# Sorting the edges of a four-layer graph network: message weights from bf16 parts, one group later, on one core

## The chip, the cores and the metric

The kernel runs on 1 core of one Trainium2 chip. The metric is the device time of one execution in microseconds (us), lower is better. The engines are TensorE (PE in the profile, its weight loads PEld), VectorE (DVE), ScalarE (ACT), GpSimd (POOL) and SyncE (SP), and DMA queues are fed from SP, ACT and POOL.

## The reference, cut to what matters

The graph has 6250 nodes of 64 features and 200000 edges. Four layers follow one another, each added to its input and normalised.

```python
# layer 0: per edge a weight of 64 numbers from a two-layer MLP on 8 + 16 edge attributes
w_ij = silu(attr8 @ W_rad1 + b_rad1) @ W_rad2 + b_rad2
w_ij += silu(attr16 @ W_sph1 + b_sph1) @ W_sph2 + b_sph2
alpha = (q[dst] * w_ij * k[src]).reshape(-1, 8, 8).sum(-1) / sqrt(8) * edge_weight[:, None]
x = layernorm(x + segment_sum(alpha[..., None] * v[src], dst) / 32)
# layer 1: three smoothing steps over the weighted edges, each with an l21 shrinkage
# layer 2: a polynomial of degree 5 in the normalised adjacency, coefficients from an MLP
# layer 3: two graph convolutions, each  adjacency @ (x W) scaled by degrees, + bias
x = layernorm(x + layer(x))            # after each
```

Everything is float32. The kernel keeps that precision on TensorE's bf16 path by splitting a float32 factor into three bf16 parts that add up to it.

## The kernel before, in words

A node is a lane (of 125) and a block (of 50). The stages run one after another, each in a block of its own with a barrier behind it:

1. `front`: makes tables of the edges' places, the projections q, k, v, and starts to fill the table `sorted_rows` in memory with zeros.
2. `sort_edges`: all 1568 tiles of 128 edges, in 196 groups of `G` = 8 tiles. Each edge gets a row of 70 numbers (64 of its weight `w_ij` times the edge weight, and six more) and a row number (the pair of its source and target block, and its rank in it), and the row is scattered there. An edge whose rank is over 128 "spills" behind the table.
3. `build_graph`: reads the sorted rows, makes one-hot matrices and counts, and layer 0's sums.
4. `spill_messages`: layer 0's messages of the spilled edges, in chunks of 125 edges, through gathers and adding scatters on GpSimd's queue; `collect` adds them.
5. `layer_norm`, `scale_of_degree` three times, `smooth` (layer 1), `coefficients` and `polynomial` (layer 2), then `project` and `convolve` twice (layer 3).

The sort is where most of the edit lies. Per group, with two buffers (`u`) for most tiles:

- SP loads, two groups ahead, `key_row` and `block_row` (both spread over the partitions) and the attributes `attrs`. It does so for group g+2 when VectorE has read `key_row` of group g (`rows_read`), and all four DMAs count on one semaphore, `loaded[u]`.
- PE, for group n (line 397 on): the hidden layer of half the group (`ps_h`, float32, 512 columns), then for each of the 8 tiles a lookup (`ps_r`, how many edges of the same block pair came before, from `hot_dt` and `count`) and a count (`ps_c`, from `hot_d` and `hot_s`). Before the next lookup, ACT must have copied `ps_c` to `count` (`snapped`). After tile 0 comes the hidden layer's other half, after tile 1 the prefix sums of the spill flags of group n-1, and with each of the tiles 4 to 7 two products with `w2` in float32 (`ps_m`); the last one counts `mixed`.
- ACT: SiLU of each half of `ps_h` into `hidden` at tiles 1 and 3, and the eight copies of `ps_c`.
- VectorE: `group_hots` (the group's table `grp`, the one-hots `hot_d`, `hot_s` and the transposed `hot_dt`, lines 455 to 464), then `places` of the group before it: eight comparisons `same` (line 483) that rank the edges in their tile, the ranks (489 to 494), the rows (497 bias added, 499 times the edge weight, 500), the spill numbers (502 to 511), which end with `row_at` and `rows_ready`.
- POOL: eight scatters for each group, one for each tile, behind `rows_ready`; `stored[u]` frees `rows[u]`.

## Time and profile before

| | |
|---|---|
| median of 3 runs | 7716.12 us (7713.63 to 7728.18) |
| profiled execution, its own time | 7703.81 us |
| its span (first to last instruction) | 7702.0 us |
| busy | PE 88%, weight loads 74%, DVE 76%, ACT 56%, POOL 32% |
| granted TensorE clock, mean | 0.964 of 2.4 GHz |
| sort stage | about 184 to 2583 us of the span |
| graph, spill stage | to about 4082, to 4137 us |
| smooth, polynomial, convolutions | to about 5840, 7050, 7671 us |

The span is one execution on the chip; the time beside it holds 1.8 us more that lies around it. Line numbers are those of the kernel before. A row of a timeline gives the start, the length, the engine and the instruction (several of a kind in a row are merged, "x4"), and in brackets how long the engine had been idle and what released it.

### The profile page before, as it was taken

The numbers are of one execution on the slowest core, as the hardware profiler recorded it, in microseconds if no ns is written. First come the engines' busy times: TensorE is split into PE (matmuls) and PEld (weight loads), VectorE is DVE, ScalarE is ACT, GpSimd is POOL, SyncE is SP. The second block draws the span as 40 slices with busy tenths as digits, with TensorE's granted clock in tenths as the row PEclk, the third lists the DMA queues.
The fourth block names the chain that finished last, engine by engine and source line by source line (L and its number), as shares of the span: only waits on it lengthen the run. The fifth ranks groups of instructions, "written<-read, shape, count | busy, mean of one in ns | idle before, by whom it ended". The sixth has DMA issues, their size and how long they took to land. (4 is left out here: it accounts for less than half of the span.)

```text
span 7702.0 us, 278354 instructions
## 1 busy us (share of the span) xinstructions
PE 6739.4 (88%) x98572; PEld 5729.8 (74%) x98572; DVE 5845.4 (76%) x17002; ACT 4337.5 (56%) x13124; POOL 2472.2 (32%) x2927
## 2 busy tenths in 40 slices
PE   2699999999999899999993898898995999998888
PEld 1455555555555699999993898897995999997878
DVE  4577777777777799898995899898897776765556
ACT  0122222222222599999993787887894666665545
POOL 0466666666666555454552000000000000000000
PEclk9999999999999999999996999999997999998979
DMA  9522222222222477666774888888894677763645
GB/s 392 181 64 64 63 63 64 64 63 62 65 64 63 138 232 233 225 229 227 231 233 155 296 322 296 305 323 288 324 344 155 203 201 203 201 197 111 196 134 157
DMA packets 629164, 1430.29 MB, mean 186 GB/s; under 512 B 248466, under 2 KB 281049, under 8 KB 624927
## 3 DMA queue, kind: packets, MB, share of 16 engines
q1 hardware_dynamic: 542480, 1234.12, 50.3%
q0 software_dynamic: 71904, 92.78, 4.2%
q10 hardware_dynamic: 14232, 96.26, 3.3%
q8 instruction: 322, 5.28, 0.3%
q14 instruction: 226, 1.85, 0.1%
HBM read 989.29 MB, written 436.68 MB: 185 GB/s over the span
## 5 line engine op out<-in xcount | busy, mean ns | idle before, releaser
L351 POOL DMA_INDIRECT sorted_rows<-sort_rows,sort_row_at x1568 | 1589.2, 1013 | 813.3 <-issue 536.0
L1637 ACT ACTIVATE smooth_msg<-smooth_ps_a,smooth_w_rows 128x64 f32<-128x64 f32 x6000 | 1308.3, 332 | 266.1 <-PE smooth_ps_a L1727 249.9
L382 ACT ACTIVATE sort_count<-sort_ps_c 50x50 bf16<-50x50 f32 x1568 | 323.1, 206 | 1807.1 <-PE sort_ps_c L414 1716.8
L1412 ACT ACTIVATE poly_cast<-poly_mat 128x1536 bf16<-128x1536 uint8 x500 | 714.8, 1475 | 441.9 <-PE poly_ps L1433 367.5
L424 PE MATMUL sort_ps_m<-sort_w,sort_hidden 128*128 128x64 f32 x3136 | 876.8, 434 | 0.0
L403 PE MATMUL sort_ps_h<-sort_attrs,sort_w 24*128 24x512 f32 x784 | 812.0, 1137 | 36.7 <-DMA sort_attrs<-in_attr_t 36.7
L1749 PE MATMUL smooth_ps_s<-smooth_msg,smooth_hot 128*128 128x64 bf16 x7500 | 771.0, 194 | 71.0 <-DVE smooth_last_part L1877 48.8
L410 PEld LDWEIGHTS sort_ps_r<-sort_count,sort_hot_dt 50*128 50x128 bf16 x1568 | 157.5, 100 | 869.7 <-issue 602.9
L1749 PE MATMUL smooth_ps_s<-smooth_rest,smooth_hot 128*128 128x64 bf16 x7500 | 766.5, 194 | 14.0 <-issue 14.0
L1749 PE MATMUL smooth_ps_s<-smooth_last_part,smooth_hot 128*128 128x64 bf16 x7500 | 765.7, 194 | 11.9 <-issue 11.9
L424 PEld LDWEIGHTS sort_ps_m<-sort_w,sort_hidden 128*128 128x128 f32 x3136 | 729.4, 324 | 40.3
L1749 PEld LDWEIGHTS smooth_ps_s<-smooth_msg,smooth_hot 128*128 128x128 bf16 x7500 | 687.6, 99 | 78.5 <-DVE smooth_last_part L1877 64.7
L763 ACT ACTIVATE graph_hot_t<-graph_ps_t 128x1024 bf16<-128x1024 bf16 x625 | 641.0, 1026 | 116.1 <-PE graph_ps_t L806 85.2
L1749 PEld LDWEIGHTS smooth_ps_s<-smooth_rest,smooth_hot 128*128 128x128 bf16 x7500 | 690.3, 99 | 19.8 <-issue 19.8
L1749 PEld LDWEIGHTS smooth_ps_s<-smooth_last_part,smooth_hot 128*128 128x128 bf16 x7500 | 686.9, 98 | 18.3 <-issue 18.3
L839 PE MATMUL graph_ps_kv<-kv_whole,graph_hot_t 125*128 125x128 bf16 x7500 | 685.9, 219 | 0.0
L1433 PE MATMUL poly_ps<-parts,poly_cast 125*128 125x192 bf16 x7500 | 639.4, 249 | 48.5 <-DVE poly_cast L1496 23.8
L1433 PEld LDWEIGHTS poly_ps<-parts,poly_cast 125*128 125x128 bf16 x7500 | 630.4, 99 | 57.1 <-issue 27.5
L1867 DVE TENSOR_TENSOR smooth_rest<-smooth_msg 128x640 f32<-128x640 f32 x750 | 615.9, 821 | 51.6 <-ACT smooth_msg L1637 34.9
L836 PE MATMUL graph_ps_q<-q_whole,graph_hot_t 125*128 (+1 forms) x7500 | 633.4, 193 | 15.1 <-ACT graph_hot_t L763 10.6
L1877 DVE TENSOR_TENSOR smooth_last_part<-smooth_rest 128x640 bf16<-128x640 f32 x750 | 614.8, 820 | 24.1 <-DVE sums_rest L1841 2.8
L733 POOL TENSOR_TENSOR graph_parts<-graph_parts 128x260 f32<-128x260 f32 x625 | 387.4, 620 | 744.6 <-DVE graph_hot L895 730.8
(342 smaller groups left out, 16117.7 us busy)
## 6 DMA issues: line engine op xcount, KB each, us to landing
poly_mat<-counts_t SPq DMA_DIRECT2D x500, 400.0 KB, 3.6
smooth_src<-src_rows SPq DMA_DIRECT2D x150, 960.0 KB, 5.0
smooth_hot<-hot_rows SPq DMA_DIRECT2D x150, 960.0 KB, 7.1
smooth_src<-src_rows SPq DMA_DIRECT2D x150, 640.0 KB, 6.1
smooth_hot<-hot_rows SPq DMA_DIRECT2D x150, 640.0 KB, 7.3
graph_edges<-sorted_rows SPq DMA_DIRECT2D x125, 700.0 KB
hot_rows<-graph_hot SPq DMA_DIRECT2D x125, 640.0 KB, 3.5
src_rows<-graph_hot_t SPq DMA_DIRECT2D x125, 640.0 KB, 3.4
```

The source lines that it names most:

```text
L351: pool.indirect_dma_start(out=sorted_rows, out_offset=bass.IndirectOffsetOnAxis(row_at[u][:, j:j + 1], 0), in_=rows[u][:, j, :], in_offset ...
L403: nc.tensor.matmul(ps_h[h][:, 0:H * ST], w1[:], attrs[u][:, h * H * ST:(h + 1) * H * ST], start=True, stop=True).then_inc(hidden_ps, 1)
L424: last = nc.tensor.matmul(ps_m[u][0:ST, t * D:(t + 1) * D], hidden[u][:, t * ST:(t + 1) * ST], w2[:], start=True, stop=True, skip_group_ch ...
L763: act.activation(hot_t[x.b][:, :, :, x.s, :].rearrange("p e t v d -> p e t (v d)"), ps_t[x.g % 2][:].rearrange("p e t v d -> p e t (v d)") ...
L836: nc.tensor.matmul(ps_q[:, 2 * t + v], d_t, q[:, i], start=i == 0, stop=i == 2, skip_group_check=True)
L839: last = nc.tensor.matmul(ps_kv[u][:, 2 * t + v], s_t, kv_parts[:, s, i], start=i == 0, stop=i == 2, skip_group_check=True)
L1412: act.activation(cast[u][h][:, DVE_S:HR, :], mat[u][h][:, DVE_S:HR, :], ACT.Copy)\
L1433: last = nc.tensor.matmul(ps[u][:, 0:3 * D], cast[u][b // HR][0:NL, b % HR, :], parts[k % 2][:, b].rearrange("p i d -> p (i d)"), start=b ...
L1637: last = act.activation(at[:, i, :], ps_a[g % 2][:, i * D:(i + 1) * D], ACT.Copy, scale=w_rows[u][:, c * CHUNK + i:c * CHUNK + i + 1])
L1749: last = nc.tensor.matmul(ps_s[u][:, 0:D], hot[u][t][:, at // 2, :, at % 2], part[:, i, :], start=False, stop=c == N_CHUNKS - 1 and i == C ...
L1867: dve.tensor_tensor(rest[c][:], msg[c][:], high(msg[c]), ALU.subtract).then_inc(firsts, 1)
L1877: dve.tensor_tensor(last_part[c][:], rest[c][:], high(rest[c]), ALU.subtract)\
```

## The change

In `sort_edges`:

- `w2` and the summed bias `b2` are split into three bf16 parts once. `hidden` is split for each group: its upper 16 bits serve as the first part where they lie (a view with a step of two), VectorE makes `hidden_rest` and `hidden_last`, two operations on 128 x 1024. The product with `w2` becomes 9 bf16 matmuls for each tile in place of one in float32, and one matmul of 3 rows and 512 columns adds the bias, so that VectorE's addition of it goes.
- These products of group n-1 are made in PE's group n, at tiles 4 to 7 (before: those of group n itself).
- `hot_dt` is made by ACT, in two activations on 50 x 1024 (|block - lane|, then relu(1 - that)), for group n+1 at tiles 5 and 6 of its group n, ahead of the copy of `ps_c` at each of them. They wait for `loaded` of group n+1.
- VectorE's order: ranks of group g, the two halves of `hidden`, the six plain columns, the spill numbers, `group_hots` of g+2, and then, behind `mixed` of g, the rows of g; `rows_ready` follows the rows. The eight `same` of g+1 come behind them.
- SP waits for `hots_t` as well before it loads the next group, and clears `y0_rows` behind the last loads.

Elsewhere: `spill_messages` takes two chunks of 125 at once (four gathers, two adding scatters that wait for each other), without clearing `y0_rows`; the three scalings of degrees share a block; `smooth` and `polynomial` split their first table in five pieces of ten blocks and let PE begin after each; `project` and the splitting ahead of each `convolve` are replaced by `conv_rows`, which goes by four blocks at a time, scales in the same pass and splits on ACT and VectorE beside PE.

```diff
@@ sort_edges, SP
                         sp.wait_ge(hidden_ps, 4 * it + (2 * u + 2))
                         sp.sem_inc(taken, 1)
+                        sp.wait_ge(hots_t, 2 * it + (u + 1))
+                        sp.sem_inc(taken, 1)
                         loads(u, bass.ds((2 * it + (2 + u)) * (G * ST), G * ST))
@@ sort_edges, ACT
+                def turned_hots(g, u, part):
+                    if part == 0:
+                        act.wait_ge(loaded[u], g * 32 + (64 - 32 * u))
+                        act.activation(lane_gap[:], block_row[u][:], ACT.Abs, bias=less_lane[0:NB, 0:1]).then_inc(gaps, 1)
+                    else:
+                        act.wait_ge(gaps, g + 1)
+                        if not isinstance(g, int) or g >= 2:
+                            act.wait_ge(based, g - 1)
+                        act.activation(hot_dt[u][:], lane_gap[:], ACT.Relu, scale=-1.0, bias=one_cols[0:NB, 0:1])\
+                           .then_inc(hots_t, 1)
...
                     for j in range(G):
+                        if j in (5, 6) and not last:
+                            turned_hots(n + 1, 1 - u, j - 5)
                         if j in (1, 3):
...
@@ sort_edges, PE
-                        if j == H:
-                            pe.wait_ge(silu, 2 * n + 2)
-                        if j >= H:
-                            for t in (2 * (j - H), 2 * (j - H) + 1):
-                                last = nc.tensor.matmul(ps_m[u][0:ST, t * D:(t + 1) * D],
-                                                        hidden[u][:, t * ST:(t + 1) * ST], w2[:], start=True,
-                                                        stop=True, skip_group_check=True)
-                    last.then_inc(mixed, 1)
+                        if j >= H and first != 0:
+                            mixes(n - 1, 1 - u, first, j - H)
+
+                def mixes(m, u, first, quarter):
+                    if quarter == 0:
+                        pe.wait_ge(halved, m + 1)
+                        if first is None:
+                            pe.wait_ge(rows_ready, m - 1)
+                        nc.tensor.matmul(ps_m[u][0:ST, :], ones[0:3, :], b2_rows[0:3].rearrange("p g d -> p (g d)"),
+                                         start=True, stop=True, skip_group_check=True)
+                    for t in (2 * quarter, 2 * quarter + 1):
+                        edges = slice(t * ST, (t + 1) * ST)
+                        for part in (high(hidden[u]), high(hidden_rest), hidden_last[:]):
+                            for i in range(3):
+                                last = nc.tensor.matmul(ps_m[u][0:ST, t * D:(t + 1) * D], part[:, edges], w2_parts[:, i, :],
+                                                        start=False, stop=True, skip_group_check=True)
+                    if quarter == G // 2 - 1:
+                        last.then_inc(mixed, 1)
@@ sort_edges, VectorE, places(g)
-                    dve.wait_ge(mixed, g + 1)
+                    dve.wait_ge(silu, 2 * g + 2)
+                    if not isinstance(g, int) or g >= 1:
+                        dve.wait_ge(mixed, g)
+                    nxt(dve.tensor_tensor(hidden_rest[:], hidden[u][:], high(hidden[u]), ALU.subtract))
+                    dve.tensor_tensor(hidden_last[:], hidden_rest[:], high(hidden_rest), ALU.subtract).then_inc(halved, 1)
                     dve.wait_ge(stored[u], 16 * G * it)
-                    nxt(dve.tensor_tensor(biased[:], ps_m[u][0:ST, :].rearrange("p (g d) -> p g d", g=G),
-                                          b2[:, 2:3, :].to_broadcast([ST, G, D]), ALU.add))
-                    dve.tensor_tensor(rows[u][:, :, 0:D], biased[:], grp[u][:, :, 2:3].to_broadcast([ST, G, D]), ALU.mult)
-                    dve.tensor_copy(rows[u][:, :, D:ROW], grp[u][:, :, 0:6])
+                    nxt(dve.tensor_copy(rows[u][:, :, D:ROW], grp[u][:, :, 0:6]))
...
-                    dve.tensor_tensor(row_at[u][:], spill_row[:], slot_row[:], ALU.add).then_inc(rows_ready, 1)
+                    nxt(dve.tensor_tensor(row_at[u][:], spill_row[:], slot_row[:], ALU.add))
+                    if with_hots:
+                        group_hots(g + 2, u)
+                    dve.wait_ge(mixed, g + 1)
+                    dve.tensor_tensor(rows[u][:, :, 0:D], ps_m[u][0:ST, :].rearrange("p (g d) -> p g d", g=G),
+                                      rows[u][:, :, W:W + 1].to_broadcast([ST, G, D]), ALU.mult).then_inc(rows_ready, 1)
@@ conv_rows, VectorE (new, in place of project and of the splitting)
+                def scale(o):
+                    dve.wait_ge(product, o + 1)
+                    s = octs[o]
+                    dve.tensor_tensor(xs[:, s, :], ps_o[o % 2][0:NL, 0:size(s) * D].rearrange("p (b d) -> p b d", d=D),
+                                      dinv[:, s].unsqueeze(2).to_broadcast([NL, size(s), D]), ALU.mult).then_inc(scaled, 1)
```

## Rows read from the trace of the kernel before

**Rows 1.** Windows: stretch, length, busy us (instructions) by engine, clock, DMA share, GB/s
```profile
400.00:2300.00 1900.00, 1779.62 (x6095) 1055.15 (x6095) 1360.78 (x6091) 444.14 (x1606) 1299.27 (x1284) 1.00 0.27 63
```

**Rows 2.** Timeline of the sort, PE through one group
```profile
1202.79 2.07 PE L403 MATMUL sort_ps_h<-sort_attrs,sort_w 24*128 24x512 f32 x2
...
1204.80 0.22 PE L410 MATMUL sort_ps_r<-sort_count,sort_hot_dt 50*128 50x50 bf16 x1
...
1209.17 0.22 PE L410 MATMUL sort_ps_r<-sort_count,sort_hot_dt 50*128 50x50 bf16 x1 [0.30 <-ACT sort_count L382]
...
1213.59 1.12 PE L424 MATMUL sort_ps_m<-sort_w,sort_hidden 128*128 128x64 f32 x4
...
1214.64 2.07 PE L403 MATMUL sort_ps_h<-sort_attrs,sort_w 24*128 24x512 f32 x2
```

**Rows 3.** Timeline, VectorE's ranks and rows, and SP's first load
```profile
1211.56 0.33 DVE L483 SCALAR_TENSOR_TENSOR sort_same<-sort_key_row,sort_grp,sort_before 128x128 bf16<-128x128 int16 x1
...
1213.75 0.07 DVE L483 DVE_READ_ACCUMULATOR sort_same<-sort_key_row,sort_grp,sort_before 128x1 f32 x1
...
1214.20 0.36 SPq L317 DMA_DIRECT2D sort_key_row<-key_rows  x1
...
1215.64 0.69 DVE L497 TENSOR_TENSOR sort_biased<-sort_ps_m,sort_b 128x512 f32<-128x512 f32 x1
```

**Rows 4.** Timeline, ACT: a SiLU half and the next copy of the counts
```profile
1208.33 0.67 ACT L379 ACTIVATE sort_hidden<-sort_ps_h,sort_b 128x512 f32<-128x512 f32 x1
...
1208.91 0.21 ACT L382 ACTIVATE sort_count<-sort_ps_c 50x50 bf16<-50x50 f32 x1
```

**Rows 5.** Timeline: first loads of two groups; VectorE released by the first one's last
```profile
270.48 0.36 SPq L317 DMA_DIRECT2D sort_key_row<-key_rows  x1
...
275.77 0.29 DVE L455 COPY sort_grp<-tbl 128x64 f32 x1 [0.93 <-DMA sort_attrs<-in_attr_t]
...
1202.20 0.36 SPq L317 DMA_DIRECT2D sort_key_row<-key_rows  x1
```

**Rows 6.** Windows of half a microsecond, in which these loads' last transfers fall
```profile
274.50:275.00 0.50, 0.50 (x5) 0.28 (x4) 0.31 (x2) 0.00 (x0) 0.26 (x1) 1.00 0.14 47
...
1206.50:1207.00 0.50, 0.50 (x1) 0.00 (x0) 0.00 (x0) 0.00 (x0) 0.50 (x1) 1.00 0.19 58
```

**Rows 7.** Groups of instructions by line: busy us, mean ns
```profile
L351 POOL DMA_INDIRECT sorted_rows<-sort_rows,sort_row_at x1568 | 1589.2, 1013 | 813.3 <-issue 536.0 <-DVE sort_row_at L511 277.0 <-DVE sort_pad_at L527 0.3
...
L379 ACT ACTIVATE sort_hidden<-sort_ps_h,sort_b 128x512 f32<-128x512 f32 x392 | 265.8, 678 | 0.0
...
L464 DVE TENSOR_SCALAR sort_hot_dt<-sort_block_row,sort_lane_col 50x1024 bf16<-50x1024 bf16 x196 | 110.7, 565 | 0.0
...
L763 ACT ACTIVATE graph_hot_t<-graph_ps_t 128x1024 bf16<-128x1024 bf16 x45 | 46.2, 1027 | 35.5 <-PE graph_ps_t L806 33.5
...
L1867 DVE TENSOR_TENSOR smooth_rest<-smooth_msg 128x640 f32<-128x640 f32 x750 | 615.9, 821 | 51.6 <-ACT smooth_msg L1637 34.9 <-DVE smooth_norm L1813 4.1 <-DVE smooth_shrink L1824 0.8
```

**Rows 8.** Timeline of the smoothing: first and last of 30 products of 64 columns
```profile
4200.81 0.20 PE L1749 MATMUL smooth_ps_s<-smooth_msg,smooth_hot 128*128 128x64 bf16 x1
...
4201.72 0.19 PE L1749 MATMUL smooth_ps_s<-smooth_last_part,smooth_hot 128*128 128x64 bf16 x1
```

**Rows 9.** Timeline of the spill stage and what follows
```profile
4096.76 0.15 DVE L1052 CAST spill_dst_at<-spill_edges 125x1 int32<-125x1 f32 x1 [13.63 <-DMA spill_edges<-sorted_rows]
...
4112.80 0.15 DVE L1052 CAST spill_dst_at<-spill_edges 125x1 int32<-125x1 f32 x1 [7.33 <-DMA spill_edges<-sorted_rows]
...
4137.40 3.60 DVE L1085 TENSOR_TENSOR node_sums<-node_sums,y 125x3300 f32<-125x3300 f32 x1 [15.95 <-PEq L53]
```

**Rows 10.** Timeline of the first projection and of the start of its convolution
```profile
7081.77 0.63 PE L575 MATMUL conv_of_ps_t<-ident,conv_of_block 125*64 125x125 f32 x2 [33.90 <-ACT conv_of_block L561]
...
7131.02 3.49 DVE L2045 TENSOR_TENSOR xs<-node_sums,dinv 125x3200 f32<-125x3200 f32 x1 [3.66 <-DMA conv_lane_col<-in_lanes]
...
7146.56 10.86 PE L1433 MATMUL conv_ps<-parts,conv_cast 125*128 125x192 bf16 x98 [19.59 <-DVE conv_cast L1496]
```

More of the change, by code:

```diff
@@ L57, in _ @@
                     sp.sem_clear(held)
+YB = NB + 1
 MOST = 112
@@ L382, in group @@
                         act.activation(count[(j + 1) % 2][:], ps_c[0:NB, 0:NB], ACT.Copy).then_inc(snapped, 1)
+                act.wait_ge(made, 2)
+                act.wait_ge(lane_ready, 1)
+                for part in two:
+                    turned_hots(0, 0, part)
                 group((0, 0), 0)
                 group((1, 1), 1)
-                with act.Fori(1, NG // 2) as it:
+                with act.Fori(1, NG // 2 - 1) as it:
                     for u in two:
                         group((2 * it + u, u), None)
+                group((NG - 2, 0), None)
+                group((NG - 1, 1), None, True)
             @blk.tensor
@@ L441, in _ @@
                 prefixes(NG)
+                for quarter in range(G // 2):
+                    mixes(NG - 1, (NG - 1) % 2, None, quarter)
             @blk.vector
@@ L446, in _, with link @@
                 dve.wait_ge(made, 2)
-                dve.tensor_tensor(b2[:, 2, :], b2[:, 0, :], b2[:, 1, :], ALU.add)
-                dve.tensor_copy(before[:], tri[:])
-                def group_hots(g, it, u, first):
-                    g_is_0 = isinstance(g, int) and g == 0
-                    dve.wait_ge(loaded[u], 64 * it + 64)
-                    if not first:
-                        dve.wait_ge(mixed, g - 1)
-                    dve.tensor_copy(grp[u][:, :, 0:8], tbl[:, bass.ds(g * G, G), :]).then_inc(step, 1)
-                    dve.wait_ge(step, 1 if g_is_0 else STEPS * g - (STEPS - 2))
+                def link(ins, value):
+                    ins.then_inc(step, 1)
+                    dve.wait_ge(step, value)
@@ L1029, in _ @@
             @blk.tensor
             def _(pe):
-                n = pe.value_load(n_spilled[0:1, 0:1], min_val=1, max_val=N_PADDED // TE + 1)
+                n = count(pe)
                 with pe.Fori(0, n) as t:
-                    pe.wait_ge(loaded, 16 * t + 16)
-                    nc.tensor.matmul(ps_id[0:TE, 0:TE], edges[:, DST:DST + 1].to_broadcast([TE, TE]),
-                                     ident[0:TE, 0:TE], start=True, stop=True).then_inc(row_ids, 1)
+                    pe.wait_ge(got, 16 * t + 16)
+                    for i in two:
+                        last = nc.tensor.matmul(ps_id[0:TE, i * TE:(i + 1) * TE],
+                                                edges[:, i, DST:DST + 1].to_broadcast([TE, TE]), ident[0:TE, 0:TE],
+                                                start=True, stop=True, skip_group_check=True)
+                    last.then_inc(row_ids, 1)
@@ L1036, in _ @@
                     pe.wait_ge(matched, t + 1)
-                    nc.tensor.matmul(ps_sum[0:TE, 0:YW], same[:], msg[:], start=True, stop=True).then_inc(summed, 1)
+                    for i in two:
+                        last = nc.tensor.matmul(ps_sum[0:TE, i * YW:(i + 1) * YW], same[:, i, :], msg[:, i, :], start=True,
+                                                stop=True, skip_group_check=True)
+                    last.then_inc(summed, 1)
             @blk.vector
             def _(dve):
-                n = dve.value_load(n_spilled[0:1, 0:1], min_val=1, max_val=N_PADDED // TE + 1)
@@ L1048, in link @@
                         ins.then_inc(step, 1)
[L1049 to L1053 removed]
+                        dve.wait_ge(step, t * STEPS + k[0])
+                    dve.wait_ge(got, 16 * t + 16)
+                    id_cols = edges[:, :, DST]
                     dve.wait_ge(row_ids, t + 1)
[L1055 removed]
@@ L1513, in pair @@
                     ahead.end()
+                before = Beside(before_vector(dve, Chain(dve, first, 0, 0), posted))
                 for u in two:
                     for h in two:
+                        before.go(1)
                         cast_half(0, 0, u, h)
+                before.end()
                 none = Beside(iter(()))
@@ L2002, in polynomial, with before_vector @@
         both = (parts, parts2)
-        def before_vector(dve, link):
+        def before_vector(dve, link, posted):
+            yield from first_parts(link, dve, posted, parts, xs, x, dis, rest)
             dve.tensor_tensor(twice[:], dis[:], dis[:], ALU.mult)
@@ L2041, in convolve, with before_vector @@
+def convolve(nc, tag, shared, ident16, out, bias, relu, dinv, xs, parts, sums, y_sb, counts):
     with ExitStack() as ctx:
         z = ctx.enter_context(nc.sbuf_tensor(f"{tag}_z", [NL, 2, D], F32))
-        def before_vector(dve, link):
-            link(dve.tensor_tensor(xs[:], h[:], wide(dinv), ALU.mult))
-            to_parts(link, dve, parts, xs, rest)
+        def before_vector(dve, link, posted):
+            dve.sem_inc(posted, NB // 2)
+            return
+            yield
         def post(dve, link, k, p):
```

388 lines of the change are left out of this document (230 added, 158 removed).

## The prediction

> **What bounds the kernel now.** I read the page first (shares by engine, the 40 slices), then windows by stage, then the timeline of each stage that the diff touches. In the sort TensorE is busy 1780 of 1900 us at full clock [rows 1]. A group has 38 PE records (8 lookups, 8 counts, 4 for the hidden layer, 16 for the mix, 2 prefix sums), so 6095 records are 160.4 groups and a group takes 1900/160.4 = 11.85 us. The timeline confirms it: hidden layer to hidden layer 1202.79 to 1214.64 [rows 2]. The reader sees one closed sequence on PE there: 2.01 to the first lookup, 4.37 to that of tile 4 at 1209.17 (with the hidden layer's other half), and 5.47 for tiles 4 to 7 with their float32 products. VectorE is busy 1361/160.4 = 8.5 us per group, ACT 2.8, POOL 8.1, so PE bounds the sort. The sort is a third of the span, everything else in the diff is start-up work of a stage. So one group's period times 194, plus small one-off terms, is the answer.
>
> **What PE gains.** The mix is now 72 bf16 matmuls and a bias matmul per group. A float32 record of the mix takes (1214.64 - 1213.59)/4 = 0.26 us, two tiles 1.05 [rows 2]. Products of 64 columns with a stationary operand loaded for each, and parts read with a step of two, go at (4201.72 - 4200.81)/29 = 0.031 us [rows 8]: 18 are 0.56. Tiles 4 to 7 would take 4 x (0.32 + 0.56) + 0.2 for the bias = 3.7 us in place of 5.47.
>
> **What the new order costs.** Let S be the start of PE's group n, just behind the last product of group n-2. A chain now runs round the loop once per group, each link waiting for the one before:
> - the last product reaches VectorE, 0.2 (a record's length [rows 8]);
> - VectorE makes the rows of n-2: one operation of 0.69 as L497 [rows 3], 0.65 as the next overlaps its end;
> - eight `same` of n-1: 1211.56 to 1213.82, 2.26 [rows 3];
> - SP sees `rows_read` and issues the loads of n+1: 0.38 [rows 3], and about 0.1 for the added wait, 0.5;
> - the loads land. From the first issue to VectorE's release 270.48 to 275.77 is 5.3 [rows 5]. In the steady part the loads issued at 1202.20 still transfer in the slice to 1207.0, and for the others release came 0.8 to 1.3 behind such a slice [rows 5, 6]: 1207.3 to 1208.3, 5.1 to 6.1. I take 5.5;
> - ACT, which stands at tile 5 of group n ahead of its count copy, makes |block - lane|. SiLU on 512 columns takes 0.678, and a copy of 1024 takes 1.027 [rows 7]; SiLU's bias makes it dearer than a copy, so I put 1024 columns with a bias at 1.10, less 0.09 overlap with the next (0.67 long, next start after 0.58 [rows 4]): 1.0. Then the count copy, 0.12 until the next starts, the relu 1.0, and the count copy of tile 6, 0.21: together 2.35;
> - PE: 0.05, lookup and count of tile 7 (1209.17 and its pair, 0.32 [rows 2]), the last 18 products 0.55.
>
> Sum 0.2 + 0.65 + 2.26 + 0.5 + 5.5 + 2.35 + 0.05 + 0.32 + 0.55 = 12.4 us, against 11.85. Before, the same load was issued just as late in VectorE's order but was wanted only by `group_hots` some 7 us later, where it had landed; now it is wanted inside the same group. What is queued behind ACT's wait is the count copy of tile 5, and PE's lookup of tile 6 waits for that.
>
> **What is hidden.** VectorE: `hot_dt` goes (0.57 [rows 7]), the bias goes (0.69), two operations of 128x1024 come. L1867 on 640 columns takes 0.82 [rows 7] and L497 on 512 takes 0.69, so 1024 take 1.22, two 2.44. They end at S + 0.2 + 0.65 + 2.26 + 1.82 (last `same` to L497 [rows 3]) + 2.5 = 7.4; PE would want them at 6.4 + 0.3. That stall of 0.7 us and all of PE's tiles 4 and 5 lie under the wait for the load, which ends at S + 9.1. VectorE's total is 8.5 - 0.57 - 0.69 + 2.44 = 9.7 busy, with gaps under 11, so it waits at the end of its loop. POOL: 8 x (1.01 [rows 7] + 0.3 between them) = 10.5 of 12.4. Take the load's lateness away, and PE's sequence is 7.4 + 0.2 + 4 x 0.88 less overlaps, 11.0: this is the cover's worth.
> The Trainium skill (ScalarE: Activation LUTs, Rules for kernel authors) says to give relu-like work to VectorE. It speaks against this change, and the rows agree: 2 x 1.10 replaces 0.57. Its price for an activation with a bias, 0.28 us and 0.833 ns per element (section What ACT_TABLE_LOAD costs), would be 1.13 and the period 12.46, the time 12 us above mine.
>
> **Sum.** Sort: 193 periods x 0.55 = +106; group 195 prepares nothing, -1; start: the loads of group 2, late behind the zero filling, now stop ACT inside group 1 rather than PE ahead of group 2, the last two links, +3; end: the last group's rows need another ranks, halves and mix, +7. Together +115.
> Spill stage: the first `got` no longer stands behind clearing `y_rows` (4096.76 came 10.7 after the stage's start, now about 3: -7.6), the second chunk's pass of 16.0 goes [rows 9], two more gathers and a second add in series return about +8.5: -15.
> Convolutions, each: the projection ran 45.6 us (7081.77 to 7127.4, just ahead of 7131.02) [rows 10]. Four blocks now cost four transposes at 0.21 [rows 10] to 0.26 and 8 records at 0.22 to 0.26 [rows 2], 2.6 to 3.1 x 12.5, plus 2 at the end: 35 to 40, -8. The splitting (7131.02 to the first product at 7146.56) leaves 3 us of waiting for the matrix: -12. Twice: -40.
> Scalings: two barriers, -2. Smoothing: VectorE is nearly full there and five pieces cost more than one (5 x 0.82 against 3.49, three such and two casts): +3. Polynomial: PE starts earlier, -1.5. Together -56.
> Net +115 - 56 = +59: span 7761, own time of such an execution 7763. The profiled execution lies 12 us under the median, so the median comes to 7716 + 59 = 7775.
>
> **Rivals.**
> A, faster: the load is hidden after all, because it lands before ACT wants it. It decides where `loaded` comes before S + 7.6, under 4 us after issue; then the period is 11.0, 194 x -0.85 + 10 - 56 = -211, 7505. The two spans of rows 5 and 6 speak against it. 0.12.
> C, a shorter chain: 0.3 off the period breaks even (59/193). The load at its lower end 5.1 and links overlapping by 0.1: 11.9, 7680. 0.17.
> B, slower: products twice as long as in the smoothing, since nine go into one PSUM range: tiles 6 and 7 then last 0.56 longer each, and of tile 6's a half still lies under ACT's wait: +0.8, 7930. 0.06. The skill (TensorE: Matmul & The Clock Gate, Back-to-back issue gap) gives 81 ns for 128 columns; by it the period would be 14.7 or less and the time 8220. The smoothing's 31 ns differ.
> D: absolute value, relu and SiLU need tables loaded anew, or the clock falls to 1.2 GHz in PE's gaps of 1.3 us: each over +250, 8000 and more. Rows 1 show clock 1.00 with such gaps. 0.03.
>
> **Numbers.** The forecast (period 12.15 to 12.8, time 7725 to 7855) holds 0.62. The range takes most of C, from 7640, and the near part of B, to 7900; about 0.8. Faster by over 0.2% (what a measurement of this kernel can tell, 15 us): A and two thirds of C, 0.23; within it 0.12 (the rest of C and the forecast's low end); slower 0.65.
>
> **What would show it.** A sort period of 12.4 by records; ACT idle ahead of |block - lane| with the release named a DMA of `attrs`, 1.5 to 2 us; PE's lookup of tile 6 waiting for `count`; VectorE idle ahead of the rows by 1 to 2 us, released by the mix; first to last product of a tile pair 0.53; spill stage to `collect` 36 us; first product of a convolution 20 us sooner. Wrong would be a DMA absent among ACT's releasers (A), or products over 0.04 us apart (B).

## The result, and the profile after

The kernel after takes 7943.7 us in the median of 4 runs (7937.66 to 7947.53), beside 7716.72 for the kernel before (7713.63 to 7728.18): a ratio of 1.029, 95% interval 1.028 to 1.0305. It is slower by 227 us, where the prediction had +59 and a range up to 7900. In four of the seven sets of experiments below the kernel before itself took about 8170 us, in the other three about 7710; they are called slow and quick sets, and versions are compared within a set.

By first and last records of each stage in the two profiled executions (spans 7936.0 and 7702.0, +234): the sort ends 269.5 us later (2852.9 against 2583.4); spill stage with `collect` -13; scalings -3; smoothing +4; polynomial and its coefficients -3; the two convolutions -24; `build_graph`, which the diff doesn't touch, +4. So the whole loss is in the sort, and all other stages together gain 35.5 us.

The page of the kernel after, slices of 198 us:

```profile
span 7936.0 us, 301350 instructions
...
PE   2688888888888879999999499899896899998888
...
PEclk9855555555555579999999699999998999999889
```

Windows of the kernel after, in the columns of [rows 1]: first two stretches inside one group, then the steady part of the sort:

```profile
1208.50:1219.80 11.30, 9.85 (x68) 5.21 (x68) 9.76 (x38) 4.78 (x11) 8.68 (x9) 0.50 0.23 66
1220.30:1223.20 2.90, 2.90 (x27) 1.50 (x26) 1.95 (x10) 0.84 (x3) 0.98 (x2) 1.00 0.06 16
400.00:2300.00 1900.00, 1608.02 (x13732) 966.31 (x13729) 1408.99 (x5479) 719.44 (x1732) 1248.15 (x1155) 0.54 0.21 57
```

The view gives a clock of 0.54 where [rows 1] had 1.00, so the first reading is that the clock fell. The records say otherwise. Timeline of PE in the kernel after, from one group's hidden layer to the next's (13.27 us in most groups, 12.66 in this one, since its end runs at 1.00):

```profile
1208.48 2.07 PE L444 MATMUL sort_ps_h<-sort_attrs,sort_w 24*128 24x512 f32 x2
...
1210.49 0.22 PE L452 MATMUL sort_ps_r<-sort_count,sort_hot_dt 50*128 50x50 bf16 x1
...
1214.86 0.22 PE L452 MATMUL sort_ps_r<-sort_count,sort_hot_dt 50*128 50x50 bf16 x1 [0.30 <-ACT sort_count L416]
1215.01 0.24 PE L456 MATMUL sort_ps_c<-sort_hot_s,sort_hot_d 128*50 128x50 bf16 x1
1215.97 0.60 PE L471 MATMUL sort_ps_m<-sort_b_rows,sort_ones 3*128 3x512 bf16 x1 [0.72 <-DVE sort_hidden_last L578]
1216.50 0.34 PE L477 MATMUL sort_ps_m<-sort_w_parts,sort_hidden 128*128 128x64 bf16 x3
1216.65 0.35 PE L477 MATMUL sort_ps_m<-sort_w_parts,sort_hidden_rest 128*128 128x64 bf16 x3
1216.81 0.35 PE L477 MATMUL sort_ps_m<-sort_w_parts,sort_hidden_last 128*128 128x64 bf16 x3
...
1220.51 0.26 PE L477 MATMUL sort_ps_m<-sort_w_parts,sort_hidden 128*128 128x64 bf16 x3
...
1220.96 0.25 PE L477 MATMUL sort_ps_m<-sort_w_parts,sort_hidden_last 128*128 128x64 bf16 x3
1221.14 1.12 PE L444 MATMUL sort_ps_h<-sort_attrs,sort_w 24*128 24x512 f32 x2
```

The same pair of hidden-layer records lasts 2.07 us at 1208.48, in the window at 0.50 (1.2 GHz), and 1.12 us at 1221.14, in the window at 1.00 (2.4 GHz). In [rows 2] it lasts 2.07, and the lookup's 0.22 is the same too. All records of that line, minimum, median and maximum in ns, first in the kernel before, then in the kernel after (whole span, and before its first recorded change of the clock):

```profile
L403 PE MATMUL sort_ps_h<-sort_attrs,sort_w x784: 1052/1133/1219, 210.2 to 2556.6; 24*128 24x512 f32 x196
```

```profile
L444 PE MATMUL sort_ps_h<-sort_attrs,sort_w x784: 587/1056/1217, 210.6 to 2816.1; 24*128 24x512 f32 x196
...
L444 PE MATMUL sort_ps_h<-sort_attrs,sort_w x20: 1052/1135/1217, 210.6 to 302.6; 24*128 24x512 f32 x20
```

In the kernel before none of 784 is shorter than 1052 ns. Of the two only the kernel after has some of 587 ns, in its short stretches at 1.00: of its records that lie wholly inside a recorded stretch, the 193 at 1.00 last 587 to 692 ns and the 544 at 0.50 last 1056 to 1217. So the kernel before sorted at 1.2 GHz from its first group to its last. The 1.00 of [rows 1] is not what the engine ran at: the first entry of the clock in its trace is at 2598.6 us, in the graph stage, and the view shows 1.00 where no entry is on record. In the kernel after the 20 records of 205 to 305 us are as long, and the view says 1.00 there too. The mean clocks of the two profiles (0.964 and 0.817) can't be compared. What keeps the engine at 1.2 GHz through this sort no run shows.

Now the prices of the mix, that is, of the products with `w2` and the bias matmul. Three products take 0.16 us at the low level (1216.50, .65, .81), 0.053 each; from 1220.51 to 1220.96, fifteen take 0.45, 0.030 each. The prediction's 0.031 came from [rows 8], a stretch at 2.4 GHz. The bias matmul takes 0.53 until the next starts, where the prediction had 0.2.

Timelines of VectorE, ScalarE and SyncE in the same group:

```profile
1208.59 0.69 DVE L595 TENSOR_TENSOR sort_rows<-sort_ps_m,sort_rows 128x512 f32<-128x512 f32 x1 [2.60 <-PE sort_ps_m L477]
1209.20 0.34 DVE L562 SCALAR_TENSOR_TENSOR sort_same<-sort_key_row,sort_grp,sort_before 128x128 bf16<-128x128 int16 x1
...
1211.49 0.57 DVE L568 TENSOR_TENSOR sort_picked<-sort_ps_r,sort_hot_s 128x400 f32<-128x400 f32 x1
...
1214.61 1.22 DVE L578 TENSOR_TENSOR sort_hidden_last<-sort_hidden_rest 128x1024 bf16<-128x1024 f32 x1
...
1212.06 0.35 SPq L329 DMA_DIRECT2D sort_key_row<-key_rows  x1
...
1216.46 1.15 ACT L394 ACTIVATE sort_lane_gap<-sort_block_row,sort_less_lane 50x1024 bf16<-50x1024 bf16 x1 [0.97 <-DMA sort_attrs<-in_attr_t]
1217.99 0.21 ACT L416 ACTIVATE sort_count<-sort_ps_c 50x50 bf16<-50x50 f32 x1 [0.38 <-PE sort_ps_c L456]
```

One closed cycle is to be seen. The last product ends, VectorE makes rows, `same`, ranks and halves (1208.59 to 1215.83), PE waits 0.72 us for them and starts the mix 7.49 us behind its group's start; the mix with the lookups and counts of tiles 5 to 7 takes 5.79 at the low level (`e2_order` below shows it undisturbed), and the next group starts: 13.28. ScalarE's wait for the load is there, as forecast, but it is 0.97 us long and ends at 1216.46, the first load having been issued at 1212.06: 4.4 us, not 5.5. And behind it the count copy of tile 5 still waits 0.38 us for PE, so nothing is held up.

### The profile page after: what moved, and what is told of

It reads as the page before. It is cut to its first block and busy times, and to the rows that moved or that the text cites. A ratio compares the mean times of both kernels' runs of the same rounds, so it can differ in the third digit from the quotient of the medians.

```text
span 7936.0 us, 301350 instructions
## 1 busy us (share of the span) xinstructions
PE 6749.8 (85%) x109744; PEld 5761.2 (73%) x109744; DVE 6081.3 (77%) x16972; ACT 4754.5 (60%) x13370; POOL 2571.6 (32%) x2927
## 5 line engine op out<-in xcount | busy, mean ns | idle before, releaser
L371 POOL DMA_INDIRECT sorted_rows<-sort_rows,sort_row_at x1568 | 1691.3, 1079 | 980.3 <-issue 542.7
L444 PE MATMUL sort_ps_h<-sort_attrs,sort_w 24*128 24x512 f32 x784 | 707.3, 997 | 1.9 <-DMA sort_attrs<-in_attr_t 1.9
L1549 DVE CAST poly_cast<-poly_mat 128x1664 bf16<-128x1664 uint8 x500 | 508.7, 1028 | 57.2 <-DMA poly_mat<-counts_t 50.6
L595 DVE TENSOR_TENSOR sort_rows<-sort_ps_m,sort_rows 128x512 f32<-128x512 f32 x196 | 135.7, 692 | 527.1 <-PE sort_ps_m L477 527.1
```

Source lines behind the costliest of these rows:

```text
L371: pool.indirect_dma_start(out=sorted_rows, out_offset=bass.IndirectOffsetOnAxis(row_at[u][:, j:j + 1], 0), in_=rows[u][:, j, :], in_offset ...
L444: nc.tensor.matmul(ps_h[h][:, 0:H * ST], w1[:], attrs[u][:, h * H * ST:(h + 1) * H * ST], start=True, stop=True).then_inc(hidden_ps, 1)
L1549: dve.tensor_copy(cast[u][h][:, 0:DVE_S, :], mat[u][h][:, 0:DVE_S, :]).then_inc(cast_v, 1)
```

## The experiments

Theory **speed**: the sort runs at 1.2 GHz in both kernels, but for short stretches in the kernel after; at that speed PE's own work is 12.49 us per group (bias matmul +0.53, products +0.11), and the new order of VectorE puts a cycle of 13.27 round it. Its rival is the prediction's **load chain**; the other, at first, that the **clock** fell and took the time with it. The experiments ran in seven sets; the kernels of one set ran on the same chip beside the kernel before, and each ratio is to its runs there. "Period" is the median distance of two groups' hidden layers.

### The order alone, the float32 mix, and the rest without the sort

`e2_order`, rows behind the first ranks:

```diff
                     dve.wait_ge(rows_read, g + 1)
+                    if not isinstance(g, int) or g >= 1:
+                        make_rows(g - 1, 1 - u)
...
+                def make_rows(g, u):
                     dve.wait_ge(mixed, g + 1)
                     dve.tensor_tensor(rows[u][:, :, 0:D], ps_m[u]...
```

> The kernel after, with the rows of group n-1 made behind the first ranks (the eight same) of group n again; parts and ScalarE's one-hots stay. Theory clock with the cycle rows, same, ranks, halves, mix: 2.26 us of same leave the cycle. At the low clock TensorE's own work (13.27 less 0.7 of waiting ahead of the mix) then bounds at about 12.5, the time about 7790; if the smaller gaps bring the clock up again, VectorE's 9.7 busy with its gaps bounds, 10.5 to 10.9, the time 7400 to 7480. Theory load chain: the loads go out 0.65 us earlier against the last product or more, so ScalarE's wait shrinks; alone that gives 11.8 at best, the time above 7650.

Measured: 7738.88 us, ratio 1.0039 (1.0024 to 1.0053). Period 12.49; 122 of 190 periods are at 12.4 to 12.6, the others, with a stretch at 2.4 GHz, at 11.0 to 12.0, mean 12.11. PE from the count ahead of the mix to the next group:

```profile
1209.61 0.24 PE L456 MATMUL sort_ps_c<-sort_hot_s,sort_hot_d 128*50 128x50 bf16 x1
1209.78 0.60 PE L471 MATMUL sort_ps_m<-sort_b_rows,sort_ones 3*128 3x512 bf16 x1
1210.32 0.34 PE L477 MATMUL sort_ps_m<-sort_w_parts,sort_hidden 128*128 128x64 bf16 x3
...
1211.39 0.22 PE L452 MATMUL sort_ps_r<-sort_count,sort_hot_dt 50*128 50x50 bf16 x1
...
1215.57 2.07 PE L444 MATMUL sort_ps_h<-sort_attrs,sort_w 24*128 24x512 f32 x2
```

What PE waits for in the sort:

```profile
PE sort_ps_r L452 <- ACT sort_count L416: 99.9, 355, 0.3
PE sort_ps_m L471 <- DVE sort_hidden_last L585: 10.8, 28, 0.5
```

The wait for the halves is all but gone (112.3 us over the same stretch in the kernel after), what is left is the count copy's 0.3 that [rows 2] have too. PE is bound by its own work, and that is 0.64 above the 11.85 of before: 0.53 for the bias matmul, and 1.07 for the 18 products of two tiles up to the next lookup (1210.32 to 1211.39), where the float32 products took 1.05. The order alone is worth about 200 us (205 by the medians, 195 by the two ratios). The mean clock of this stretch reads 0.53, lower than after's 0.54, and the kernel is quicker all the same: the reading that a fall of the clock made the loss doesn't stand.

`e3_f32mix`, the order of the kernel after, the mix in float32, the bias still a matmul:

```diff
-                        for part in (high(hidden[u]), high(hidden_rest), hidden_last[:]):
-                            for i in range(3):
-                                last = nc.tensor.matmul(..., part[:, edges], w2_parts[:, i, :], ...
+                        last = nc.tensor.matmul(..., hidden[u][:, edges], w2[:], start=False, ...
```

> The kernel after, but the mix multiplies in float32 as in the kernel before (8 products instead of 72 in bf16; VectorE makes no halves); the bias matmul, the order of VectorE and ScalarE's one-hots stay. Theory clock (it fell because the mix asks less of TensorE and because of the new waits): clock 1.00 and a period bound by TensorE at 11.85 to 12.0 us, the time 7680 to 7720 with the other stages 36 us shorter. Theory load chain: period 12.4 here too, the time about 7790. If the clock falls here as well, the cause is not the bf16 products but the new order or ScalarE's one-hots: the float32 products then take twice as long and the time is over 8500.

Measured: 7801.43 us, ratio 1.0119 (1.0102 to 1.0136), period 12.38. The load chain had 12.4 and seemed confirmed. It isn't: PE's timeline has no wait but the count copy's, the mix starts 0.17 behind the count of tile 4, and 12.38 is 11.85 + 0.53 for the bias matmul. ScalarE waits 1.05 us for the load (issued 1206.20, operation at 1210.68, 4.5 us), and PE doesn't notice. This run also shows the clock's trap: the window reads 1.00 with records of the low level.

```profile
L444 PE MATMUL sort_ps_h<-sort_attrs,sort_w x784: 1052/1135/1217, 210.5 to 2667.9; 24*128 24x512 f32 x196
...
400.00:2300.00 1900.00, 1784.91 (x5979) 1023.52 (x5978) 1133.97 (x5522) 733.03 (x1841) 1212.00 (x1227) 1.00 0.22 61
```

`e4_rest`, the function `sort_edges` of the kernel before in the kernel after (with the clearing of `y0_rows` behind its loads):

> The change without its sort: the loop that sorts the edges is that of the kernel before, all other stages are those after. From the two profiles the other stages differ by 234 - 269.5 = -35.5 us, of which convolutions -24, spill stage -13, smoothing +4, graph +4, polynomial and scalings -6. Expected: 7681, and a sort of 11.85 us per group at clock 1.00. The prediction's own number for these stages was -56, which would give 7661.

Measured: 7677.99 us, ratio 0.9959 (0.9946 to 0.9971), period 11.85. The rest gives 30 us by the medians, 35.5 by the profiles, not 56.

### More work for PE, fewer products

`e5_fill`, with `FILL = {1: 6, 2: 1, 3: 1, 4: 6}` (14 matmuls in a group) and, ahead of the first of them, a wait for `rows_ready` of group n-2:

```diff
+                        for _ in range(FILL.get(j, 0) if first is None else 0):
+                            nc.tensor.matmul(ps_m[1 - u][0:ST, 0:448], ones[:], b2_flat[:, 0:448], ...
```

> The kernel after, with 14 extra bf16 matmuls of 448 columns per group on TensorE (six ahead of the prefix sums, one behind each count of tiles 2 and 3, six ahead of the mix); nobody reads what they write. New reading of the profiles: the sort ran at 1.2 GHz in the kernel before too, since its hidden-layer records last 1052 to 1219 ns there (median 1133), 1056 in the median of the kernel after, and 587 only in the latter's short stretches at 2.4 GHz; the 1.00 in the view of before is no record. Theory speed: at 1.2 GHz a product takes 0.053 us and the bias matmul 0.53, so TensorE's own work is 12.5 and the cycle of VectorE and mix 13.27. If the extra matmuls bring the engine to 2.4 GHz, hidden-layer records last 0.59 to 0.69, the cycle of rows to halves (7.2) and mix (3.6, and 0.3 of hand-overs) gives 11.1 to 11.3 and the time about 7550; theory load chain would give 12.4 even then. If they don't, their 14 x 0.38 us add 4 us to each group: 17.3, the time about 8730.

`e6_order_six`, `e7_after_six` (the same edit, without the first's new order) and `e8_order_six_fill`:

```diff
-                        for part in (high(hidden[u]), high(hidden_rest), hidden_last[:]):
-                            for i in range(3):
+                        for n_w, part in ((3, high(hidden[u])), (2, high(hidden_rest)), (1, hidden_last[:])):
+                            for i in range(n_w):
```

> The kernel after with the rows behind the first ranks (as e2_order), and six products for each tile in place of nine: the last part of hidden goes with the first part of the weights alone, the middle one with the first two; the three smallest products, under 2 to the -24 of the result, are left out. Theory speed (TensorE bound at 1.2 GHz, a product 0.053 us): 12.49 of e2_order less 24 x 0.053 = 11.2 us per group, the time 7739 - 196 x 1.27 + what e2_order had gained in its short stretches at 2.4 GHz (12.49 against a mean of 12.12: up to 72) = 7490 to 7560. Theory that VectorE or GpSimd already bounds in e2_order: unchanged, 7740.

> The kernel after in its own order, with six products for each tile in place of nine (the same three left out). Theory cycle (VectorE's rows, same, ranks and halves, 7.25 us, then the mix, and nothing of one beside the other): 13.27 less 24 x 0.053 = 12.0 us per group, the time about 7944 - 230 = 7710. Theory that TensorE's own work alone bounds: 11.2, about 7550. Theory load chain: not under 12.4, 7790.

> e6_order_six with seven extra bf16 matmuls of 448 columns per group (three ahead of the prefix sums, one behind each count of tiles 2 and 3, two ahead of the mix). If the engine then runs at 2.4 GHz: VectorE's own 10.6 us (rows to the last same in e2_order) and its hand-over bound, 10.6 to 10.9, the time 7400 to 7450, hidden-layer records 0.59 to 0.69. If it stays at 1.2 GHz: 11.2 and the extra matmuls beyond the 0.75 that they fill, 13.1 or more, the time about 7850 or more.

In this set the kernel before itself took 8177.58 us (8130 to 8199). Measured: 8618.91 (ratio 1.056), 8365.06 (1.025), 8438.57 (1.034) and 8476.25 (1.039), periods 16.53, 15.23, 15.87 and 16.20. The forecasts, made for a kernel before of some 7708 us, can't be held against these times. `e5_fill` still tells something: the clock from 400 to 2300 us reads 0.62, hidden-layer records go down to 587 ns but their median stays 1056. The kernel after in a set of this kind (`e15_after`, below) has none under 1052. So the extra matmuls brought the engine to 2.4 GHz in stretches, and not for good; what the new sort would take at 2.4 GHz throughout stays unmeasured. `e8_order_six_fill` never left 1.2 GHz (records of 1052 to 1217). The six products could not be judged here, and were run again.

### The six products again, and the one-hots alone

`e9_order_six` and `e10_after_six` are the kernels of `e6` and `e7`. `e11_hots_only` takes from the new sort everything but ScalarE's one-hots: float32 mix as in `e3_f32mix`, order as in `e2_order`, and

```diff
-                        nc.tensor.matmul(ps_m[u][0:ST, :], ones[0:3, :], b2_rows[0:3]...
...
+                    dve.tensor_tensor(biased[:], ps_m[u][0:ST, :]..., b2[:, 2:3, :]..., ALU.add)...
```

> The kernel of e6_order_six once more (rows behind the first ranks, six products), because in the call before all kernels, that of before too (8178 us in place of 7708), were held up by late transfers and late fetches. Theory speed (TensorE bound at 1.2 GHz): 12.49 of e2_order less 24 x 0.053 = 11.2 us per group and 7490 to 7560. Theory that VectorE (10.6 from rows to the last same) or GpSimd (10.5) bounds: 10.6 to 12.1, and TensorE waits ahead of the mix or ahead of a group's first lookup.

> The kernel of e7_after_six once more (the order of the kernel after, six products). Theory cycle (VectorE's rows to halves, 7.25, then the mix, nothing of one beside the other): 13.27 - 1.27 = 12.0 us, the time about 7710. Theory that TensorE's own work alone bounds: 11.2, as e9_order_six, about 7550. Theory load chain: 12.4, 7790.

> The kernel after with the rows behind the first ranks, the mix in float32 and the bias added by VectorE as in the kernel before; of the sort's change only ScalarE's one-hots (and the lookahead in VectorE's hots) stay. Theory speed: TensorE's own work is that of before, 11.85 us at 1.2 GHz, the time that of e4_rest, 7678; then the bias matmul alone costs 0.53 us per group (12.38 of e3_f32mix), the products 0.11 more (12.49 of e2_order), the order 0.78 (13.27). Theory that ScalarE's one-hots cost something by themselves (their wait for the load, 1.05 us in e3_f32mix): up to 12.4, 7785.

| | us | ratio (interval) | period, expected by speed | measured |
|---|---|---|---|---|
| `e9_order_six` | 7567.86 | 0.9821 (0.9805 to 0.9838) | 11.2 | 11.21 |
| `e10_after_six` | 7717.49 | 1.0013 (1.0004 to 1.0023) | 12.0 | 11.99 |
| `e11_hots_only` | 7685.48 | 0.9973 (0.9963 to 0.9983) | 11.85 | 11.85 |

All three periods come out to 0.01 us. With the prices of the low level the cycle and PE's own work are two separate terms: taking 24 products of 0.053 away takes 1.27 from either, and the order is worth 0.78 with six products as with nine. A period under 12.4 in the order of the kernel after (`e10`) speaks against the load chain as a bound, and PE's waits decide it: ScalarE waits for the load in all 158 groups, 164.6 us in all, and PE's waits for the count's copy are still none longer than 0.3 us:

```profile
ACT sort_lane_gap L394 <- DMA sort_attrs<-in_attr_t: 164.6, 158, 1.6
...
PE sort_ps_m L471 <- DVE sort_hidden_last L578: 114.0, 158, 0.7
PE sort_ps_r L452 <- ACT sort_count L416: 94.1, 316, 0.3
```

For `e9_order_six` the agreement is weaker evidence than it seems. GpSimd's stores fill its sort too, and ask for the same period: 1356 of them in 1900 us, 11.21 for eight, with 1.2 us of waiting for rows. In `e10` GpSimd waits 170.3 us for rows, in `e11` 266.1.

```profile
L371 POOL DMA_INDIRECT sorted_rows<-sort_rows,sort_row_at x1356 | 1449.3, 1069 | 452.7 <-issue 451.5 <-DVE sort_rows L554 1.2
```

ScalarE's one-hots alone cost nothing that is measured and give nothing: the period is that of before.

### The bias matmul in PE's idle time

`e13_gap_bias` builds on `e9_order_six` (`e12_gap_bias` is the same with `start=True` in both halves and leaves a part of the bias out of the sum; it took 8371.47 beside 8172.0, period 15.25, and tells no more than the next). The two halves stand in place of the one matmul ahead of the mix:

```diff
+                        if j in (2, 3) and first != 0:
+                            bias(n - 1, 1 - u, first, j - 2)
...
+                def bias(m, u, first, half):
...
+                    at = slice(half * 256, half * 256 + 256)
+                    nc.tensor.matmul(ps_m[u][0:ST, at], ones[0:3, :], ..., start=half == 0, ...
```

> e9_order_six with the bias matmul cut into two of 256 columns, issued behind the counts of tiles 2 and 3, where TensorE stands idle 0.30 us each for a count's copy, in place of one of 512 columns (0.53 us) ahead of the mix. Theory speed (TensorE's own work at 1.2 GHz bounds): 11.21 - 0.53 = 10.68 us per group, if VectorE (10.6 from rows to the last same, 0.2 for its wake by the mix) leaves it; so 10.7 to 10.85, the time 7568 - 196 x 0.36 to 0.53 = 7465 to 7500. If a matmul of 256 columns takes more than the 0.30 of idleness, or VectorE or GpSimd (8 x 1.3) binds first, 11.0 or more, 7530.

> The kernel of e12_gap_bias (six products, rows behind the first ranks, the bias matmul as two of 256 columns in TensorE's idle 0.30 us behind the counts of tiles 2 and 3), the second of them now adding to what the first began, once more because the call before ran where the kernel before itself took 8172 us. Theory speed (TensorE's own work at 1.2 GHz bounds): 11.21 - 0.53 = 10.68 us per group, or VectorE's 10.6 with 0.2 for its wake by the mix: 10.7 to 10.85, 1.75 to 2.2% under e9_order_six's 0.982 of the kernel before at most, so a ratio of 0.969 to 0.973. If a matmul of 256 columns takes more than the 0.30 of idleness, or VectorE or GpSimd (8 x 1.3) binds first: 11.0 or more, a ratio of 0.977.

Measured: 8364.4 beside 8168.29, ratio 1.0246, period 15.23: as `e6_order_six`, which has the bias matmul whole. `e14_gap_bias` and `e16_gap_bias` are the same kernel, `e15_after` and `e17_before` the two kernels of this case once more.

> The kernel of e13_gap_bias. Where the kernel before takes about 7710: 10.7 to 10.85 us per group and a ratio of 0.969 to 0.973 by theory speed; 11.0 or more and 0.977 if the half matmuls don't fit TensorE's idle 0.30 us or VectorE or GpSimd binds. Where the kernel before takes about 8170, something other than these engines binds, as in the three calls before: about 15.2 us per group and 1.025, as e6_order_six and e13_gap_bias alike.

> The kernel after, unchanged, beside the kernel before on the same chip. Theory speed, where the kernel before takes about 7710: ratio 1.029 again, 13.27 us per group. Where the kernel before takes about 8170: if the late transfers and fetches bind there whatever TensorE does, the same 15.2 us per group and 1.025; if they add to TensorE's cycle, 16.6 or more and 1.06.

Measured, with the kernel before at 8196.64: 8367.11 (ratio 1.021, 1.0165 to 1.026) and 8595.56 (1.0495, 1.0446 to 1.0544); periods 15.23 and 16.45. So in the sets in which all kernels are slow the period still depends on the order (`e7` against `e6`, 0.64) and on the products (`e15` against `e7`, 0.58), but not on the bias matmul's 0.53 (`e14` against `e6`). The kernel after loses its time there in the sort: between its two profiles the sort's end moves by 653.8 us and the span by 656.8. Timeline of ScalarE in `e14_gap_bias`:

```profile
1213.11 1.14 ACT L394 ACTIVATE sort_lane_gap<-sort_block_row,sort_less_lane 50x1024 bf16<-50x1024 bf16 x1
1216.27 0.21 ACT L416 ACTIVATE sort_count<-sort_ps_c 50x50 bf16<-50x50 f32 x1 [2.02 <-remote]
1216.41 1.15 ACT L399 ACTIVATE sort_hot_dt<-sort_lane_gap,sort_one_cols 50x1024 bf16<-50x1024 bf16 x1
1220.13 0.21 ACT L416 ACTIVATE sort_count<-sort_ps_c 50x50 bf16<-50x50 f32 x1 [2.56 <-remote]
```

Behind each one-hot operation the count's copy starts 2.0 and 2.6 us late, released by something that the profile calls remote; 4.6 us per group that no profile of a quick set has. It is so in the whole stretch from 400 to 2300 us: all 237 such waits of `e14` stand directly behind one of the two one-hot operations, and so do all 202 in `e6`, all 122 in `e15` and 125 of 134 in `e7`. But the kernel before, whose ScalarE has no such operations, is slow in these sets too, by some 470 us; `e17_before` was to show where, and ran in a quick set. So what releases the copies, and what slows the kernel before, stays open. The expectations speak of late transfers and late fetches. By the packets of the traces the last transfer of a group's loads ends 4.25 us behind the first issue in `e6` and 3.89 in `e9` (medians), 0.36 us apart where the periods are 4.0 apart; in `e15` and the kernel after it is 3.59 and 3.89. Late fetches are seen in no trace.

> The kernel of e14_gap_bias. Where the kernel before takes about 7710: TensorE's own work is 10.68 us per group and VectorE's 10.8 with its wake; but in the profile of e9_order_six GpSimd's eight indirect stores already fill the group (starts 1.27 apart, some records of 1.5 to 2.0 us), so 10.8 to 11.2 and a ratio of 0.969 to 0.982. Where the kernel before takes about 8170: 15.2 and 1.02 to 1.025.

> The kernel before, for its profile on this chip. Where it takes about 7710: 11.85 us per group. Where it takes about 8170: 14.2 us per group (470 us over 196 groups more); if ScalarE's pauses of 2.0 and 2.6 us for a count's copy, which in e14_gap_bias stand behind the two one-hot operations, come from those operations, they aren't here; if they come from the chip (whatever releases the copy late), they are, one or two in a group.

Measured, with the kernel before at 7718.55: `e16_gap_bias` 7568.63, ratio 0.9798 (0.9782 to 0.9814), period 11.26, mean 11.22; `e17_before` 7709.75, period 11.85. The 10.7 by PE's and VectorE's sums did not come: the bias matmul is out of PE's way, and the interval overlaps that of `e9_order_six` (0.9805 to 0.9838). GpSimd binds. Its one line in the window from 400 to 2300, then what waits behind it:

```profile
L371 POOL DMA_INDIRECT sorted_rows<-sort_rows,sort_row_at x1352 | 1439.0, 1064 | 461.4 <-issue 461.4
```

```profile
DVE sort_rows L594 <- DMA sorted_rows<-sort_rows,sort_row_at: 91.9, 132, 2.3
...
PE sort_ps_m L482 <- DVE sort_hidden_last L592: 55.6, 118, 0.9
```

1439.0 busy and 461.4 between stores make up the 1900 us, and it waits for no engine: 1900/1352 = 1.405 us per store, eight are 11.24. VectorE waits for its stores before it fills the rows again, and PE waits for VectorE's halves behind that. In the kernel after GpSimd waits 322 us for rows in the same stretch. This and `e9_order_six` are the best versions found in the quick sets: about 2% under the kernel before and 4.6 to 4.8% under the kernel after. In the slow sets the same two are 2.1 to 2.5% above the kernel before.

## Why the prediction was wrong, point by point

- **Direction**: right, slower, and by luck, since the forecast had it from a chain that doesn't bind. The size is +227 in place of +59.
- **The step that failed**: "What PE gains". It put 18 products at 0.56 (0.031 each, from the smoothing) and the bias at 0.2, and so tiles 4 to 7 at 3.7 us in place of 5.47. Measured: 0.95 for the products, 0.12 more until the next lookup starts, 0.53 for the bias, and tiles 4 to 7 at 6.1. A gain of 1.8 was a loss of 0.64. The cause is the first paragraph's "at full clock": a price read at 2.4 GHz was set against records made at 1.2. Rows 2 held the contradiction, since two hidden-layer records of 512 float32 columns took 2.07 there; nothing at 2.4 GHz was laid beside it. The Trainium skill (TensorE: Matmul & The Clock Gate, Back-to-back issue gap) gives for a cold engine and a matmul by itself, without the load of its weights, a gap of the columns divided by 1.2 GHz, which for 64 columns is an estimate of 53 ns. The products of this trace, each with its own load, agree with it at 0.053 us; the bias matmul's 512 columns took 0.53 us, where the same estimate is 0.43. The 81 ns for 128 columns that rival B weighed stand in the same section of the Trainium skill.
- **"What is hidden"**: the halves end at S + 7.35 (forecast 7.4), PE waits 0.72 for them (0.7). Both right. But the wait was booked as covered by ScalarE's, and it is exposed. With the measured price of the mix this paragraph's own sum would have given 7.4 + 5.79 = 13.2 in place of 11.0, and with it the bound that was found, 13.27.
- **"What the new order costs"**: the chain exists, link by link: rows 0.61 until the next (0.65), `same` 2.3 (2.26), the load's issue 0.6 later (0.5), one-hot operations 1.15 (1.0 to 1.1). The landing is 4.4 (5.5, bounds 5.1 to 6.1), outside its bounds: one reading came from the start of the sort, the other from windows in which transfers still ran, and neither dates the landing of these four loads in the steady part. The chain then ends too early to bind. `e10` shows that it doesn't bind at 11.99, and `e3`'s 12.38 agrees with it by chance.
- **Rivals**: A's condition was not met, since the load came at S + 7.98 and 4.4 us after issue (before S + 7.6, under 4), and its effect came all the same: nothing waits for the load, because the mix is longer than forecast. Its time is wrong, since its 11.0 used the same price; whether it would hold at 2.4 GHz no run shows. B (dear products, +0.8) is the nearest in mechanism: its sign, products over 0.04 us apart, was met with 0.053, though for another reason than the one it named, and it has 7930. D said that the clock falls in PE's gaps, or that tables are loaded anew. The view of the clock seems to show the first, and the records refute it; `e2` and `e9` to `e11` leave it nothing. Of the second there is no trace: both profiles have five ACT_TABLE_LOADs.
- **Sort**: 7 us of start (3), 192 periods of +1.32 in the mean (0.55), 8.5 of end (7): 269.5. The mean is 13.17, under the 13.27, for the short stretches at 2.4 GHz.
- **Other stages**: spill -13 (-15), scalings -3 (-2), smoothing +4 (+3), polynomial -3 (-1.5): right. Convolutions -24 (-40): the mechanism holds, the first product comes 53.5 us behind the layer norm before it in place of 72.3, 18.8 sooner (20). But then VectorE's casts wait for the matrix, which the splitting used to cover: eight of the first nine groups of them are released by a load, and over both convolutions these waits are 42.9 us in place of 10.8. Of the 18.8 us a convolution keeps 12; that the other 7 go to these waits is likely, and no run shows it by itself.

```profile
7384.56 2.04 DVE L1549 CAST conv_cast<-conv_mat 128x1664 bf16<-128x1664 uint8 x2 [5.97 <-DMA conv_mat<-counts]
...
7403.97 1.03 DVE L1549 CAST conv_cast<-conv_mat 128x1664 bf16<-128x1664 uint8 x1 [3.02 <-DMA conv_mat<-counts]
```

## What to carry to other kernels

Before a price is carried from one stage to another, lay one record of the same form from both beside each other: if a 512-column matmul takes twice as long in one, the stages run at different clocks, whatever the view of the clock says. At 1.2 GHz, nine bf16 products of 64 columns cost PE as much here as one float32 product (1.07 us against 1.05 for two tiles), and splitting paid only once three of the nine were left out and the order was mended. And of an order on one engine, ask which two engines it makes take turns: the rows ahead of the ranks cost 0.78 us because `same`, which needs nothing of the mix, then stood between mix and mix.

## What the runs showed of the hardware that was not expected

- The granted clock reads 1.00 until its first recorded change, also where every matmul lasts as long as at 1.2 GHz (784 hidden-layer records of 1052 to 1219 ns before; 587 to 692 in the stretches recorded at 2.4 GHz after).
- A PE that is busy 94% of the time [rows 1] stayed at 1.2 GHz for the 2.4 ms of the sort. With 14 extra matmuls of 448 columns per group the mean reading was 0.62, and it was at 2.4 GHz in stretches only.
- In four of the seven sets the kernel before took 8168 to 8197 us in place of 7706 to 7719, and ratios moved with it (the kernel after 1.0495 in place of 1.029, the six products in the better order 1.025 in place of 0.982). Whether it lies in the chip or in the moment is not shown: of the sets that name chip 4 two are quick and two slow. A version is to be judged only beside runs of the kernel before from the same set.
- Eight indirect stores of 128 rows from GpSimd take 11.24 us, 1.405 each with what lies between, where they wait for no rows (`e16_gap_bias`).
